# A fused two-layer perceiver step on one core: the query map's scale moved from the cube into the quotient of the linear attention

## The reference

```python
def _focused_feature_map(x, scale):
    x = jax.nn.relu(x) + EPS
    x = x / scale
    x_norm = jnp.linalg.norm(x, axis=-1, keepdims=True)
    xp = x ** 3
    return xp / jnp.linalg.norm(xp, axis=-1, keepdims=True) * x_norm

q = _focused_feature_map(input_q @ Wq + bq, sp)      # and k from the context
z = 1.0 / (einsum('bhic,bhc->bhi', q, k.sum(axis=2)) + 1e-6)
kv = einsum('bhjc,bhjd->bhcd', k, v)
x = einsum('bhic,bhcd->bhid', q, kv) * z[..., None]
```

## Time and profile before

| | |
|---|---|
| median of 3 runs | 2232.66 us (2227.91 to 2236.93) |
| profiled execution, device time | 2231.95 us |
| its span, first to last instruction | 2230.2 us |
| second loop in it | from about 1416 us to the end, some 814 us |
| busy share of the whole span | PE 84%, DVE 71%, ACT 66%, POOL 54% |
| mean granted TensorE clock | 0.914 |

### The profile page before, as it was taken

The page is one execution under the profiler, slowest core; times in us unless marked ns, Lnnn a source line. Parts: engine busy times, 40 slices in busy tenths (PEclk is TensorE's granted clock), DMA queues, the critical chain, the costliest instruction groups (busy, mean ns, idle before and its releaser), DMA issues. The chain is left out here.

```text
span 2230.2 us, 41590 instructions
## 1 busy us (share of the span) xinstructions
PE 1871.8 (84%) x14324; PEld 1256.8 (56%) x14355; DVE 1590.7 (71%) x2945; ACT 1480.0 (66%) x3431; POOL 1210.8 (54%) x1300
## 2 busy tenths in 40 slices
PE   4998999999899899898898855478888888988874
PEld 2665555565565465565565512356676767666652
DVE  3458777867768768677677784557878787888873
ACT  2568878878878778778778764124666565656654
POOL 1435546555545545556555532246777677777751
PEclk8999999999999999999999977678989898989975
DMA  7321121211112121121120110100000000000000
GB/s 186 116 89 62 60 73 50 77 62 60 60 62 78 53 69 60 53 69 62 60 69 22 43 43 10 52 8 7 15 10 12 12 12 12 12 12 12 10 9 10
DMA packets 48370, 103.20 MB, mean 46 GB/s; under 512 B 6384, under 2 KB 25072, under 8 KB 43376
## 3 DMA queue, kind: packets, MB, share of 16 engines
q1 hardware_dynamic: 48240, 101.57, 14.4%
HBM read 93.03 MB, written 8.52 MB: 46 GB/s over the span
## 5 line engine op out<-in xcount | busy, mean ns | idle before, releaser
L862 POOL TENSOR_TENSOR kcube<-kcube,ksq 128x512 f32<-128x512 f32 x128 | 179.0, 1399 | 463.7 <-ACT ksq L719 463.7
L697 ACT ACTIVATE abuf<-delta,cols 128x496 f32<-128x496 f32 x512 | 339.7, 702 | 30.6 <-DVE gP L944 14.4
L872 POOL TENSOR_TENSOR yac<-yac,gP 128x1024 f32<-128x1024 f32 x128 | 302.5, 2363 | 11.5 <-ACT gP L706 10.4
L944 DVE TENSOR_TENSOR_SCAN gP<-abuf,ps_s 128x512 f32<-128x512 f32 x256 | 293.5, 1197 | 0.6 <-POOL yac L872 0.6
L524 PE MATMUL ps_kv<-kcube,cx 128*128 128x256 f32 x1024 | 245.5, 383 | 32.1 <-ACT Gs L745 29.2
L944 DVE TENSOR_TENSOR_SCAN gL<-abuf,ps_s 128x512 f32<-128x512 f32 x192 | 223.3, 1207 | 57.3 <-ACT abuf L697 57.3
L512 PE MATMUL ps_kv<-w_k,cT 128*128 128x256 f32 x1024 | 263.4, 401 | 0.0
L570 PE MATMUL ps_t<-gL,diag 128*128 128x512 f32 x384 | 195.0, 633 | 54.3 <-DVE gL L944 49.0
L524 PEld LDWEIGHTS ps_kv<-kcube,cx 128*128 128x128 f32 x1024 | 190.8, 191 | 78.2 <-issue 50.8
L512 PEld LDWEIGHTS ps_kv<-w_k,cT 128*128 128x128 f32 x1024 | 189.4, 195 | 51.9 <-issue 30.1
L583 PE MATMUL ps_kv<-hT,w_pT 128*128 128x512 f32 x384 | 187.0, 610 | 19.1 <-ACT delta L770 14.6
(11 more groups left out here) (312 smaller groups left out, 4255.7 us busy)
## 6 DMA issues: line engine op xcount, KB each, us to landing
cT<-in_h_ctxT SPq DMA_DIRECT2D x32, 1028.0 KB, 4.9
cx<-in_ctx SPq DMA_DIRECT2D x32, 1024.0 KB, 5.4
xT<-in_h_xT SPq DMA_DIRECT2D x8, 512.0 KB, 3.9
xcur<-in_x SPq DMA_DIRECT2D x32, 128.0 KB, 2.0
x_mid<-xb SPq DMA_DIRECT2D x16, 256.0 KB, 2.2
x_c<-x_mid SPq DMA_DIRECT2D x32, 128.0 KB, 2.0
out<-y SPq DMA_DIRECT2D x32, 128.0 KB, 1.7
kv_all<-vleft SPq DMA_DIRECT2D x8, 256.0 KB, 10.7
```

The lines of the kernel that those rows point to most:

```text
L697: act.activation(abuf[q % 2][:, i, :].rearrange("p (b t) -> p b t", t=T)[:, :, 1:T], delta[J % 2][:, :].rearrange("p (b t) -> p b t", t=T) ...
L862: pool.tensor_tensor(t[:, :, :], t[:, :, :], ksq[:, :, :], ALU.mult).then_inc(S["k3_ready"], 1)
L872: pool.tensor_tensor(yac[:, :, :], yac[:, :, :], pool_home(q)[:, :, :], ALU.add).then_inc(S["pacc_done"], 1)
L944: dve.tensor_tensor_scan(dst[:, i, :], abuf[q % 2][:, i, :], ps_u[:, :], 0.0, ALU.mult, ALU.add).then_inc(S["scan_done"], 1)
```

## The change

The cube is no longer scaled. PE transposes the raw cube, as soon as POOL has formed it (`d_k3` in place of `d_qf`), and multiplies it. The two sums of squares swap their places in `s26`, so that the same two powers give |x^3| and 1/|x|. POOL multiplies them into one number per token, `d_is` = 1/r, in an added instruction behind the roots with a wait of its own for `d_r` and one for `d_dz`. DVE's instruction L1644 is gone. Its `dz` (L1681) becomes a scalar_tensor_tensor that forms d_is x 1e-6 + denominator and waits for `d_qf`, which POOL's new instruction now raises. Moving `bl` and `ksb` in the source changes no instruction.

```diff
@@ PE
         if d2 is not None:
-            pe.wait_ge(S["d_qf"], d2 + 1)
+            pe.wait_ge(S["d_k3"], d2 + 1)
             turn(ps_d, qcube[:, :], DC, ident[:, :]).then_inc(S["d_qturn"], 1)
@@ ACT
-            act.activation(ksq[:, :], kq[:, :], ACT.Square, accum_out=sm["s26"][:, 0:1]).then_inc(S["d_s2"], 1)
+            act.activation(ksq[:, :], kq[:, :], ACT.Square, accum_out=sm["s26"][:, 1:2]).then_inc(S["d_s2"], 1)
...
-            act.activation(ksq[:, :], qcube[:, :], ACT.Square, accum_out=sm["s26"][:, 1:2]).then_inc(S["d_s6"], 1)
+            act.activation(ksq[:, :], qcube[:, :], ACT.Square, accum_out=sm["s26"][:, 0:1]).then_inc(S["d_s6"], 1)
@@ POOL
             pool.wait_ge(S["d_s6"], d1 + 1)
             pool.tensor_tensor(sm["rr"][:, :], sm["s26"][:, :], roots[:, 3:5], ALU.pow).then_inc(S["d_r"], 1)
+            pool.wait_ge(S["d_r"], d1 + 1)
+            if d2 is not None:
+                pool.wait_ge(S["d_dz"], d2 + 1)
+            pool.tensor_tensor(sm["d_is"][:, :], sm["rr"][:, 0:1], sm["rr"][:, 1:2], ALU.mult).then_inc(S["d_qf"], 1)
@@ DVE
-        if d2 is not None:
-            dve.wait_ge(S["d_r"], d2 + 1)
-            dve.tensor_scalar(qcube[:, :], qcube[:, :], sm["rr"][:, 0:1], sm["rr"][:, 1:2], ALU.mult, ALU.mult).then_inc(S["d_qf"], 1)
...
             dve.wait_ge(S["d_num"], d2 + 1)
-            dve.tensor_scalar(halves(dz[:, :]), halves(ps_d[:, 0:DC * (P + HH)])[:, :, P:P + HH], K_EPS, None, ALU.add).then_inc(S["d_dz"], 1)
+            dve.wait_ge(S["d_qf"], d2 + 1)
+            dve.scalar_tensor_tensor(out=halves(dz[:, :]), in0=sm["d_is"][:, 0:1].unsqueeze(1).broadcast_to([P, DC, HH]), scalar=K_EPS,
+                                     in1=halves(ps_d[:, 0:DC * (P + HH)])[:, :, P:P + HH], op0=ALU.mult, op1=ALU.add).then_inc(S["d_dz"], 1)
```

More of the change, by code:

```diff
@@ L1313, in main2 @@
     blk = sb("blk", [P, GB, DC, P + HH])
+    bl = blk[:, :, :, :].rearrange("p b c n -> p (b c) n")
     z, dz, den_z = (sb(n, [P, H]) for n in ("z", "dz", "den_z"))
@@ L1330, in main2 @@
     sm = {n: sb("sm_" + n, [P, w]) for n, w in dict(
-        c_bn=6, c_mv=2, c_ve=1, g_ve=1, d_ve=1, e_ve=1, f_ve=1, h_ve=1, c_r=1, g_bn=12, g_mv=2, g_r=1, d_bn=6, d_mv=2, d_r=1, s26=2, rr=2, e_bn=6, e_mv=2, e_r=1,
+        c_bn=6, c_mv=2, c_ve=1, g_ve=1, d_ve=1, e_ve=1, f_ve=1, h_ve=1, c_r=1, g_bn=12, g_mv=2, g_r=1, d_bn=6, d_mv=2, d_r=1, s26=2, rr=2, d_is=1, e_bn=6, e_mv=2, e_r=1,
         f_ms=1, f_mx=1, f_r=1, f_m=1, f_i=1, f_qs=1, f_ds=1, h_ms=1, h_mx=1, h_r=1, h_m=1, h_i=1, h_qs=1, h_ds=1).items()}
@@ L1574, in pool_body @@
             kvb = kv_all[:, ds(d1 * GB, GB), :, :].rearrange("p b c n -> p (b c) n")
-            ksb = ks_all[:, ds(d1 * GB, GB), :].rearrange("p b c -> p (b c)")
-            bl = blk[:, :, :, :].rearrange("p b c n -> p (b c) n")
             pool.tensor_tensor(bl[:, :, 0:P].rearrange("p g (e d) -> p g e d", d=HD),
@@ L1580, in pool_body @@
                                ALU.mult).then_inc(S["d_blk"], 1)
+            ksb = ks_all[:, ds(d1 * GB, GB), :].rearrange("p b c -> p (b c)")
             pool.tensor_tensor(bl[:, :, P:P + HH], ksb.unsqueeze(2).broadcast_to([P, GB * DC, HH]),
```

## The result

The changed kernel takes 2215.92 us (median of 5 runs, 2209.78 to 2218.15) against 2232.66; the ratio is 0.9919, with a 95% interval of 0.9896 to 0.9942. It is faster by 16.7 us, twice the 8.2 us that the forecast (2224.5) stood for, and inside the stated range of 2214 to 2242.

What follows compares the result with a forecast made beforehand. The second loop's pass was bounded by the chain x3, POOL's roots, he, PE's middle, x5, with a 21.58 us floor plus low-clock time. Terms 0.2 - 2.2 - 0.5 - 5.5 = -8.0 gave 2224.5 us; 80% range 2214 to 2242.

Steps and rivals of the forecast that it cites:

- the circle: Second loop: x3, x_p, POOL's roots, he, PE's middle, kTm, x5, c_proj, x3 was said to set the pass.
- L1644 at 0: DVE behind x3: removing 0.41 us per pass gains 0, since the wait for root h covers it; uncovered, 12.7 us.
- PE's earlier start at 0: PE's first transpose starts about 0.85 us earlier behind c_proj; PE then waits longer for he, gain 0.
- x_p at -0.07: POOL's x_p loses its DVE neighbour, 0.797 to 0.727 us, over 31 passes: -2.2 us.
- dz was put at +0.05: DVE's two-source dz gets 0.05 us longer, on the circle in a few passes only: +0.2 us in all.
- The ends of the loop: Near the loop's end, stages behind DVE's wait for the roots move forward in a few passes: -0.5 us.
- The clock's term: PE's low-clock stretches in the second loop: one long stretch in five becomes short, -5.5 us; ends -12.6 and +16.2.
- the stretches begin later with PE's work: PE's low-clock stretches were to begin 0.4 to 0.85 us later in the pass, the shift of PE's work.
- a stretch is long because it begins early: Low-clock stretches beginning at 3.92 and 4.39 us behind x3 are short, those at 3.76 and before long.
- the clock no longer falls in most passes: Rival on PE's clock: passes like the 21.58 us one, -19.3, with the rest -21.8, giving 2211 us; chance 0.07.
- The slower rival: PE's longer sparse part from x3 + 0.4 to he makes low-clock stretches long, giving 2246 us; chance 0.13.
- the 0.41 us would come off the pass: Rival: x3, L1644, L1647, statistics, he is the true chain, -12.7 and -0.5, giving 2219.5 us; chance 0.07.

Runs made afterwards that it cites:

- junk_later: Changed kernel plus an unread 0.41 us cube scaling on DVE behind pT_s and the statistics, before root h; 2217.58 us, ratio 0.9940 to the kernel before.
- hold_all: Changed kernel with an unread cube scaling where L1644 stood and PE's transposes waiting for it; 2230.80 us, ratio 0.9986 to the kernel before.
- dve_only: Changed kernel with an unread cube scaling on DVE where L1644 stood, PE's transposes not waiting for it; 2230.97 us, ratio 0.9992 to the kernel before.
- att_late: Changed kernel with PE's attention products held back from x3 + 1.35 to x3 + 1.88; 2213.09 us, ratio 0.9915 to the kernel before.
- before_pad: Kernel before with one more 128x1 product on POOL behind x_p; 2243.67 us, ratio 1.0055.
- turn_late: Changed kernel with the cube's transposes moved behind the attention products in PE's order; 2225.18 us, ratio 0.9968 to the kernel before.
- pool_pad: Changed kernel with one more 128x1 product on POOL behind x_p; 2229.99 us, ratio 0.9992 to the kernel before.
- after_fillAB: Changed kernel plus three unread PE products behind the cube's transposes and three in the wait for he; 2214.49 us, ratio 0.9920 to the kernel before.
- after_fillA: Changed kernel plus three unread PE products directly behind the cube's transposes; 2213.66 us, ratio 0.9927 to the kernel before.
- before_fill3: Kernel before plus three unread PE products behind L1369, in the wait for he; 2222.68 us, ratio 0.9954.

## Why the prediction was right, and where not

*The terms on the circle were right.* L1644 at 0: junk_later has its 0.41 us in the same pass and the same second loop of 768.7. PE's earlier start at 0: its waits for pT_s and he grew instead, to 1.16 and 1.26 (1.36 was forecast; he came 0.07 earlier with x_p). d_is at 0 in POOL's wait, 0.195 for 0.19. x_p at -0.07: 0.797 to 0.727, he and the full-clock pass 0.07 to 0.08 earlier. The GPSIMD Engine Reference of the Trainium skill (Specifications) names contention with a neighbour in a two-port mode; the times agree with it, but no trace shows the mode of L1644. dz was put at +0.05 and came out at -0.005: a mis-sized term of no weight. The ends of the loop, put at -0.5, gave nothing that shows: the second loop lost 17.9, its 21 full passes 18.2.

*The clock's term failed in size and in its mechanism.* The prediction took -5.5 us, from "I expect the low stretches to begin later in the pass ... One long stretch in five then becomes short". Measured is -16.5 in the same 21 passes: the long ones are gone, and two passes of three have no fall. Two steps behind it failed. The first was that the stretches begin later with PE's work. The one kind left begins at 4.15 to 4.36 us behind x3, where the short ones of the kernel before stood too (3.92 and 4.39); between hold_all and dve_only, with the transposes 1.03 us apart, the starts are the same to 0.06 in the passes with all stages, and the lengths are the same. The second was that a stretch is long because it begins early. It was read off five stretches; in att_late one that begins at 2.80 is short, in the kernel before one at 2.86 is long. With the transposes in front and the attention products late the mean pass is 22.26 (dve_only) or 21.61 (att_late), and place does not tell these apart. What the runs show in its place is a pattern that changes with a few hundredths of a microsecond between x3 and he, and so of the full-clock pass, and at 21.50 with the place of the transposes as well:

| kernel | full-clock pass | he behind x3 | transposes | mean of 21 passes |
|---|---|---|---|---|
| before | 21.58 | 4.53 | behind L1644 | 22.50 |
| before_pad | 21.72 (none seen; 21.58 + 0.14) | 4.67 | behind L1644 | 22.74 |
| hold_all | 21.54 | 4.49 | behind the extra scaling | 22.26 |
| dve_only | 21.54 | 4.49 | in front | 22.26 |
| turn_late | 21.50 | 4.45 | behind the attention products | 22.10 |
| after | 21.50 | 4.46 | in front | 21.63 |
| junk_later | 21.50 | 4.45 | in front | 21.62 |
| att_late | 21.50 | 4.45 | in front | 21.61 |
| pool_pad | 21.64 | 4.59 | in front | 22.18 |

So the small term, x_p's 0.07 us, priced at 2.2, seems to be a lever for the large one: without the transposes in front (turn_late) the mean pass goes from 22.50 to 22.10, with them in front to 21.63. I had taken both terms as independent and added them.

That 2215.9 lies in the 80% range is in part luck. The forecast's own range, 2217 to 2230, does not hold it, and by the prediction's own bounds the outcome is "faster" (under 2221.5), which had 0.31, and not "same", which had 0.58.

*The rivals.* Closest to what happened was the last, that the clock no longer falls in most passes (2211, chance 0.07). Its reason was the longer dense run with the transposes in front. That is at most a part: it did nothing in dve_only, and counts between turn_late and the changed kernel. The slower rival, that the longer wait of PE for he would keep the clock down, did not come. The prediction had named a rule of the Trainium skill (TensorE: Matmul & The Clock Gate, HAM oscillation), that idle time of PE between bursts of products lets the clock be throttled again. The fillers agree with it: with work in those waits the clock is 1.00 over 22 passes (after_fillAB). What the prediction made of it, a longer last wait and so more falls, does not hold in this change: the wait went from 1.01 to 1.26 and the falls became fewer. That the 0.41 us would come off the pass (2219.5) gave the nearest time of all, 3.6 us off, for a wrong reason; without junk_later it could have passed for the explanation.

*What stays open.* That the 0.04 us of x_p is what parts dve_only from the changed kernel is argued by elimination (junk_later, att_late), not shown by a run that changes x_p alone. Nor do the runs tell whether it is the length of the pass that counts or that of its sparse part, from x3 to he: every run that changed the one changed the other by the same amount, as the table shows, and none lengthened the pass behind he. Which lengths give few falls I can't forecast: +0.14 brought falls back in the changed kernel, and 0.79 less, with the fillers of after_fillA, took them all away; the two parts of that last run were not tried apart.

## What to carry to other kernels

Where the granted clock differs from pass to pass in a repeating pattern, measure the full-clock pass and the mean pass apart: the first answers to the instructions, the second also to the pattern. Here 0.08 us less on the circle, with the transposes in front, moved the mean pass by 0.87. Then don't add the clock's term to the others as if it were independent; give it the whole span, from all passes at the floor to all as dear as the dearest. And look at what stands on one engine between two links of the circle: an instruction whose inputs are ready before the link, like root g, can be put ahead of it, and that was worth more than the change itself.

## What the runs showed of the hardware

- POOL's 128x256 sum took 0.727 us with a 32-bit transpose of DVE beside it (after), 0.797 where a scaling of the same size that writes its own source ran beside its first 0.2 us (before), and 0.766 where that scaling wrote to another tile (dve_only).
- DVE's scalar_tensor_tensor on 16 columns with one source in PSUM and one broadcast from a single SBUF column took 0.151 us, no more than the one-source form at 0.156.
- A fall of the clock can be free: in att_late a pass with a 3.4 us stretch at 1.2 GHz took 21.49 us; it began 2.78 us behind x3. In the changed kernel one of the same length, begun at 4.16, cost 0.36, and in before_fill3 one that met the added products cost 1.06.
- In every kernel looked at, PE stood idle once or more near the entry of the loop for 1.3 to 2.3 us with no wait that the profile shows ("issue"): once in before and after, three times in after_fillAB. What brings these on was not tested.
